# Third attention of a perceiver kernel: scores first in a tick, the constant and the values' products set between turnings, values' projections two ticks sooner for the first four tiles

## The reference, cut to what matters

```
xn = layernorm(x) * norm_g + norm_b
q = xn @ Wq                      # 16 heads of 64
k, v = split(x @ Wkv)
k, v = two constant ("null") keys and values, then k, v
q, k = l2norm(q) * q_scale, l2norm(k) * k_scale
sim = q @ k^T * 8 + slopes * -|distance|, causal
x = x + softmax(sim) @ v @ Wout
```

## Time and profile before

| what | value |
|---|---|
| median of the 3 runs shown | 3663.85 us (3663.14 to 3670.09) |
| the profiled execution's own time | 3666.37 us |
| its span, first to last instruction | 3664.6 us |
| PE, share of the span | 91% |
| DVE | 59% |
| ACT, POOL | 35%, 29% |
| mean granted TensorE clock | 0.944 of full speed |

### The profile page before, as it was taken

The page is one execution under the profiler, slowest core; times in us unless marked ns, Lnnn a source line. Parts: engine busy times, 40 slices in busy tenths (PEclk is TensorE's granted clock), DMA queues, the critical chain, the costliest instruction groups (busy, mean ns, idle before and its releaser), DMA issues.

```text
span 3664.6 us, 93827 instructions
## 1 busy us (share of the span) xinstructions
PE 3323.7 (91%) x39692; PEld 2731.6 (75%) x39692; DVE 2160.9 (59%) x5264; ACT 1292.4 (35%) x3205; POOL 1062.4 (29%) x1653
## 2 busy tenths in 40 slices
PE   7988739988997979999999979989999999998996
PEld 6876638546985757777777757777888878887895
DVE  5766553355676145555555467745444448887557
ACT  6863101233221213333333443314223236666221
POOL 6658215122003433222222243210000025554102
PEclk9989859998996989999999989989999999999997
DMA  5620249461003321111111100003112111112000
GB/s 163 182 79 3 67 142 283 140 198 47 3 3 127 89 75 53 46 43 46 47 47 47 51 6 3 3 3 122 59 69 92 60 43 51 49 49 65 3 3 27
DMA packets 211282, 246.58 MB, mean 67 GB/s; under 512 B 19412, under 2 KB 191184, under 8 KB 207920
## 3 DMA queue, kind: packets, MB, share of 16 engines
q1 hardware_dynamic: 203376, 230.34, 19.8%
q0 software_dynamic: 7488, 10.23, 1.5%
HBM read 221.46 MB, written 18.61 MB: 66 GB/s over the span
## 4 chain that ended last, share of the span: by engine, by line
PE 75%; DVE 11%; issue 6%; POOL 3%; ACT 3%; DMA 1%; SPq 0%; DVEq 0%; ACTq 0%; POOLq 0%
PE psum L189 45%; PE psum L3631 11%; PE psum L991 2%; PE psum L3881 2%; PE psum L963 2%; PE psum L3110 2%; PE psum L3211 1%; PE psum L3179 1%; PE psum L3871 1%; PE psum L976 1%; DVE l2a_ss L1659 1%; DVE g_xn L258 1%; PE psum L3120 1%; POOL l0a_ms L1191 1%; PE psum L3111 1%
## 5 line engine op out<-in xcount | busy, mean ns | idle before, releaser
L245 POOL TENSOR_SCALAR g_rs<-g_mv 128x4 f32<-128x4 f32 x24 | 4.9, 206 | 780.3 <-DVE g_mv L378 779.8
L3631 PE MATMUL psum<-l2f_hhi,l2f_whi 128*128 128x512 f32 x512 | 199.4, 389 | 0.0
L3631 PE MATMUL psum<-l2f_hlo,l2f_whi 128*128 128x512 f32 x512 | 199.4, 389 | 0.0
L3631 PE MATMUL psum<-l2f_hhi,l2f_wlo 128*128 128x512 f32 x512 | 199.3, 389 | 0.0
L189 PE MATMUL psum<-l2x_kT,l2x_Qp 128*128 128x257 f32 x768 | 179.1, 383 | 2.6 <-ACT g_xn L3523 2.6
L189 PE MATMUL psum<-g_xn,l2x_tok 128*128 128x384 f32 x512 | 177.7, 489 | 1.4 <-ACT g_xn L3532 1.4
L3685 DVE CAST l2f_hhi<-l2f_tmp 128x512 fp32r<-128x512 f32 x96 | 41.0, 427 | 202.0 <-ACT l2f_tmp L3748 200.9
L189 PEld LDWEIGHTS psum<-l2x_kT,l2x_Qp 128*128 128x128 f32 x768 | 142.1, 192 | 21.5 <-issue 3.0
L189 PEld LDWEIGHTS psum<-g_xn,l2x_tok 128*128 128x128 f32 x512 | 93.4, 190 | 56.8 <-issue 2.6
L3748 ACT ACTIVATE l2f_tmp<-psum,g_cols 128x512 f32<-128x512 f32 x64 | 44.2, 690 | 240.1 <-PE psum L3631 240.1
L389 DVE TENSOR_TENSOR g_x<-g_x,psum 128x256 f32<-128x256 f32 x128 | 53.1, 416 | 127.4 <-PE psum L189 124.2
(11 more groups left out here) (871 smaller groups left out, 10511.0 us busy)
## 6 DMA issues: line engine op xcount, KB each, us to landing
l2f_raw<-L2f_h SPq DMA_DIRECT2D x64, 512.0 KB, 3.2
l0f_w<-L0f_w SPq DMA_DIRECT2D x23, 1024.0 KB, 8.0
l0x_ctxT<-ctxT SPq DMA_DIRECT2D x64, 257.0 KB, 2.8
l1x_ctxT<-ctxT SPq DMA_DIRECT2D x64, 257.0 KB, 6.0
l0x_ctok<-ctx SPq DMA_DIRECT2D x64, 256.0 KB, 3.2
l1x_ctok<-ctx SPq DMA_DIRECT2D x64, 256.0 KB
l2x_cT<-ctxT SPq DMA_DIRECT2D x64, 256.0 KB, 2.8
l2x_tok<-ctx SPq DMA_DIRECT2D x128, 128.0 KB, 2.9
```

The lines of the kernel that those rows point to most:

```text
L3631: t = e.matmul(z, a, b, start=c == 0 and u == 0, stop=c == 7 and u == 2)
```

## The change

Six things, all in `l2_attn`: (1) PE's list starts with the scores; (2) on PE the constant product stands between the two turnings, and the values product behind the second; (3) project comes behind values; (4) the value products of tiles 0 to 3 are run with lag 2 (ticks 2 to 5) and those of the rest with lag 4 as before, on PE and on ACT; (5) DVE moves `qT` out, then does top, then moves `kT` out, and p1b stands ahead of total; (6) DVE does outT before divide, ACT does outT before the keys.

```diff
             def p1v(i):
+                w.wait_ge(norm.low.at(8))
                 w.wait_ge(w_lo.at(6))
...
-            ticks(16, {(0, "q"): lambda i: p1(i, 0), (0, "k"): lambda i: p1(i, 1), (4, "v"): p1v, (0, "null"): null,
+            ticks(16, {(0, "q"): lambda i: p1(i, 0), (0, "k"): lambda i: p1(i, 1), (0, "null"): null,
+                       (0, "v"): lambda i: p1v(i - 2) if 2 <= i < 6 else None, (4, "v"): lambda i: p1v(i) if i >= 4 else None,
                        (2, "q"): lambda i: p2(i, 0), (2, "k"): lambda i: p2(i, 1), **at.pe(e, w, banks, ready)},
-                  [(2, "q"), 3, (2, "k"), (7, "constant"), 8, (0, "k"), 7, (4, "v"), (0, "null"), (0, "q")])
+                  [3, (2, "q"), (7, "constant"), (2, "k"), 7, 8, (0, "k"), (4, "v"), (0, "v"), (0, "null"), (0, "q")])
...
-            ticks(16, {(0, "q"): lambda i: p1(i, 0), (0, "k"): lambda i: p1(i, 1), 1: p1b, 2: p2,
-                       (0, "later"): later, **at.dve(e, w, banks)},
-                  [2, 3, 8, 1, 6, (0, "k"), 7, (0, "q"), (0, "later")])
+            ticks(16, {(0, "q"): lambda i: p1(i, 0), (0, "k"): lambda i: p1(i, 1), 1: p1b,
+                       (2, "q"): lambda i: p2(i, 0), (2, "k"): lambda i: p2(i, 1), (0, "later"): later, **at.dve(e, w, banks)},
+                  [(2, "q"), 3, (2, "k"), 1, 8, 7, 6, (0, "k"), (0, "q"), (0, "later")])
...
-                       **at.act(e, w, banks)}, [2, 5, (0, "k"), 7, (4, "v"), (0, "q"), (0, "later")])
+                       **at.act(e, w, banks)}, [2, 5, 7, (0, "k"), (4, "v"), (0, "v"), (0, "q"), (0, "later")])
```

More of the change, by code:

```diff
@@ L1666, in p1b, with p2 @@
                 e.tensor_tensor(d, d, f.unsqueeze(2).to_broadcast([128, 32, 64]), ALU.mult).then_inc(*qn_ok.up())
-            def p2(i):
-                for n in (0, 2):
+            def p2(i, a):
+                for n in [2 * a]:
                     w.wait_ge(turned.at(4 * i + n + 1))
-                    o = (qT[i % 2][:].rearrange("p c (j q) -> p c j q", j=4), kT[i % 2][:, :, :, 2:34])[n // 2]
+                    o = (qT[i % 2][:].rearrange("p c (j q) -> p c j q", j=4), kT[i % 2][:, :, :, 2:34])[a]
                     e.tensor_scalar(o[:, 0:4], banks.of(("T", i, n))[:].rearrange("p (c j q) -> p c j q", c=4, j=4),
                                     K.col(("L2_attn_q_scale", "L2_attn_k_scale")[n // 2], 0), None, ALU.mult).then_inc(*T_dve.up())
-            ticks(16, {(0, "q"): lambda i: p1(i, 0), (0, "k"): lambda i: p1(i, 1), 1: p1b, 2: p2,
-                       (0, "later"): later, **at.dve(e, w, banks)},
-                  [2, 3, 8, 1, 6, (0, "k"), 7, (0, "q"), (0, "later")])
+            ticks(16, {(0, "q"): lambda i: p1(i, 0), (0, "k"): lambda i: p1(i, 1), 1: p1b,
+                       (2, "q"): lambda i: p2(i, 0), (2, "k"): lambda i: p2(i, 1), (0, "later"): later, **at.dve(e, w, banks)},
+                  [(2, "q"), 3, (2, "k"), 1, 8, 7, 6, (0, "k"), (0, "q"), (0, "later")])
         def act(e):
@@ L1718, in p2 @@
                                  scale=K.col(("L2_attn_q_scale", "L2_attn_k_scale")[n // 2], 0)).then_inc(*T_act.up())
-            ticks(16, {(0, "q"): lambda i: p1(i, 0), (0, "k"): lambda i: p1(i, 1), (4, "v"): p1v, 2: p2, (0, "later"): later,
-                       **at.act(e, w, banks)}, [2, 5, (0, "k"), 7, (4, "v"), (0, "q"), (0, "later")])
+            ticks(16, {(0, "q"): lambda i: p1(i, 0), (0, "k"): lambda i: p1(i, 1), (4, "v"): lambda i: p1v(i) if i >= 4 else None,
+                       (0, "v"): lambda i: p1v(i - 2) if 2 <= i < 6 else None, 2: p2, (0, "later"): later,
+                       **at.act(e, w, banks)}, [2, 5, 7, (0, "k"), (4, "v"), (0, "v"), (0, "q"), (0, "later")])
         K.layer(sp, pe, pool, dve, act)
```

## The result

The changed kernel takes 3684.99 us (median of 9 runs, 3680.30 to 3691.35); the kernel before, on the same chip, 3667.93 us (9 runs, 3649.72 to 3676.51). The ratio is 1.0053, with a 95% interval of 1.0035 to 1.0071: slower by 0.5%. The forecast was 3672 us, with a range up to 3684. The sign is that of the likeliest outcome; the size, +17.1 us between the medians, is twice what was forecast, and the time lies 1 us outside the range. That last us is no more than chance: the kernel before measured 4 us more here than the 3663.85 that the forecast was added to.

The account below looks back on a forecast made before the run. The prediction saw a PE-DVE loop as the bound, becoming POOL and DVE's 18.8 us round in middle ticks. Terms -7.9 + 6.2 + 6.5 + 3.2 = +8.0 us on 3663.85 gave 3672 us, range 3660 to 3684.

Parts of the forecast that it names:

- the likeliest outcome: Whole kernel: slower by over 0.2%, chance 0.49.
- early ticks: Ticks 2 to 6: key product waits for DVE's later keys' eviction, value product makes PE late; +6.2 us, ends 0 and +9.8.
- middle ticks: Tile 7's to tile 15's power: POOL and DVE set a round of 18.8 us; -7.9 us, ends -11.3 and 0.
- last ticks: Tick 16 on: values stand inside the round between constant and project; +6.5 us, ends +5.0 and +8.0.
- clock: TensorE's clock in early and last ticks: one full tick more at 1.2 GHz; +3.2 us, ends 0 and +9.6.
- The first rival: PE is the bound everywhere, middle round 18.38 us; together -10.4 us, 3653 us, faster; chance 0.10.
- the 2.5 us wait of the constant product: Last ticks: PE waits some 2.5 us in each 11.8 us round, in three earlier ticks of the end.
- the third rival: Clock falls in early and last ticks, three ticks more at 1.2 GHz: +14.4 us, 3678 us, up to 3684; chance 0.19.

Follow-up runs that it names:

- filler_early: The changed kernel with 16 idle 512-column products in each of ticks 3 to 6, around the keys' turning where PE waits: 3684.72 us, ratio 1.0056.
- one filled round: From the changed kernel with 8 or 20 idle 512-column products where PE waits in four of the last ticks: 3684.93 us, ratio 1.0053.
- keys_out_first: The changed kernel with DVE moving both turned banks out before top: 3680.47 us, ratio 1.0038.
- pe_order_only: The kernel before with only two PE moves, scores first and constant between the turnings: 3654.41 us, ratio 0.9976.
- pe_order_values_first: The kernel before with scores first, constant between the turnings and values ahead of project on PE: 3700.76 us, ratio 1.0106.
- wide_between: pe_order_values_first plus 12 idle 256-column products between the keys' turning and values in ticks 8 to 15: 3692.51 us, ratio 1.0078.
- project_before_values: The changed kernel with project ahead of values on PE again: 3690.14 us, ratio 1.0069.

## Why the prediction was right about the order and wrong about the size

| term | forecast | waits | as measured, two executions |
|---|---|---|---|
| early ticks | +6.2 | +6.3 (`filler_early`) | +10.6, +11.3 |
| middle ticks | -7.9 | -8.7 (8 x 18.7 = 149.6) | -0.2, -5.4, with 2.5 and 2.4 us of pauses |
| last ticks | +6.5 | not seen whole; one filled round 11.8, as forecast | +15.0, +11.4 |
| clock | +3.2 | | 11 to 19 in all (estimate) |

**The early term was right.** The key product's wait for DVE's late eviction, 1.78 us, and the powers' distances of 16.5 show it step by step, the distances in `filler_early`. Undoing the eviction's place (`keys_out_first`) gives 99.5.

**The middle round was right**: 18.7 against 18.8, with DVE waiting 2.42 us for POOL. The first rival (18.38, PE the bound) is refuted by that. It is the wait that shows the mechanism and not the number: `pe_order_only` has rounds of 18.7 too, with DVE's old order and PE waiting 0.41 us for DVE's keys. So DVE's new order brought nothing in the middle, which the forecast did not ask.

**The last ticks' round was right at full rate**, 11.8 us in the one round seen so, and the 2.5 us wait of the constant product too.

**The step that failed is the clock's term**, "I take +3.2 us, one such tick in all; the ends are 0 and +9.6". The waits add up to 6.3 - 8.7 + 6.5 = +4.1 (the 6.5 is the forecast's own); the executions show +17.3 and +25.4, so 13 to 21 us are left over. About 2 us of that are the middle's pauses that the trace gives to nobody, for which the forecast had no term. The rest, 11 to 19 us, is what the clock costs, by this estimate: three to six times the term and above its upper end. Three things were wrong in it. First, the middle was left out: I read the granted 1.00 there as "there is nothing left to gain" and did not ask what could be lost. But the change joins scores, turning, constant, turning and values to 7 us of small products, where before project and the key product stood ahead of values, and a pause of PE can now fall behind or into such a run. `pe_order_values_first` shows the cost of it where such a wait comes every tick: 21 us in the middle. Second, the third rival, which has the clock right, had three more slow ticks at 3.2 us; the trace has three slow key products early (1.7 to 2.4 us each), three slow rounds in the middle, and every tick of the end. It deserved more than its 0.19, and a price per place rather than per tick. Third, what I held against that rival, early products at full rate after waits of 1 us and more, was half of what the old kernel shows: its early stretch has a granted clock of 0.89, and its first key product there takes 4.29 us from start to start instead of 2.90.

The Trainium skill (TensorE: Matmul & The Clock Gate, "A second HAM failure mode: psum-queue depth-cycling") tells of a clock that swings between its two rates when PE idles briefly and often. The early ticks here agree: 2.77 and 1.78 us of waits, then 5.29 us for 2.90. The middle agrees in part: its average, PE 97% busy (153.67 of 158.12 us) at a granted clock of 0.95, hides that each slow round has a pause of 1.0 us or more ahead of the fall. But pauses as frequent do not always do it: `wide_between` waits 1.2 us in each tick with the clock at 0.99, the kernel before 1.06 us at 1.00.

**What stays open.** Why one execution has two slow projects in the middle and the next one none or one is not settled, nor why the same wait leaves two projects of `project_before_values` at full rate and slows six, nor whether the shape of the small products matters: the runs vary the wide work and the waits, not the small products. What the pauses are that the trace gives to nobody (0.3 to 1.5 us, several in some middle stretches) is not known. The part of the end's +11.4 to +15.0 that the waits make is inferred from one filled round and the forecast's count, not seen in an execution at full rate throughout. And no filled kernel was faster as a whole than the changed one, so the clock's cost is shown by stretches and not by a median. The DVE and ACT orders of the change were not tried alone on the kernel before.

## What to carry to other kernels

When an order is written anew for an engine that is nearly always busy, price the clock as a term of its own: write down PE's sequence and look for waits that fall into or behind a stretch of only small products (here 5 to 7 us of them and a pause of 1.2 us); a wide product between them, or work in the wait, is cover for the clock as other work is cover for a wait. A wait soon after wide products did no harm here. A granted clock of 1.00 in the old order says that there is nothing to win, not that there is nothing to lose. And if a change has six parts, try the cheap ones alone: here two moves on PE were worth -0.24%, and the rest of the change turned that into +0.5%.

## What the hardware showed that I had not expected

- PE's busy share does not tell its clock: 97% busy went with a granted 0.95 in the middle after and 95% with 0.86 in `pe_order_values_first`, but 94% with 0.99 in `wide_between` and 93% with 1.00 in the kernel before. Where the wait stands tells more: 1.06 us soon after wide products cost nothing, 1.2 us behind 5 us of small ones slowed six projects of eight (`project_before_values`), and 0.41 us there did not.
- Work that nobody needs can shorten a stretch: 11 us of idle wide products made the middle of `pe_order_values_first` 10 us shorter (176.5 to 166.4 us).
- The clock can fall in the middle of a wide product, 1.2 us after its start (2355.56 to 2356.76), so the product that runs slowly need not be the one to blame; here a pause of 1.50 us stood ahead of it.
